# The gates of a final block in two turns of 128 nodes on one PSUM bank, and a fourth bank for the count products

## The chip, the core and the metric

The kernel runs on one core of a Trainium2 chip. The metric is the device time of one execution in microseconds (us), as the median of several runs; lower is better.

## The reference

One round of message passing over a graph of 12,500 nodes and 200,000 edges, a GRU cell, a residual and a layer normalization. The edges are sorted by destination, and the destinations are skewed: `dst = 12500 * u**2` with u uniform, so the first nodes have many edges each and the last ones few.

```python
src_h = h[src] @ W_msg.T + b_msg                       # h is x, [12500, 128] f32
msg = src_h + edge_embed[clip(edge_type, 0, 8)]
messages = segment_sum(msg, dst, 12500)
gi = messages @ W_ih.T + b_ih                          # [12500, 384], chunks r, z, n
gh = h @ W_hh.T + b_hh
r = sigmoid(i_r + h_r); z = sigmoid(i_z + h_z)
n = tanh(i_n + r * h_n)
h_new = (1 - z) * n + z * h
out = layernorm(x + h_new)
```

## The kernel before

The products with the weights are moved behind the sum over edges, so each node needs only the sum of its sources' rows of x and a count of its edge types. Two methods build the sums.

**Dense part (nodes 0 to 3327).** For each slot of 128 edges VectorE (DVE) writes two one-hot tables, `ohk` and `ohl` (lines 862 to 872, four slots at a time, "B" in the item list), and TensorE (PE) multiplies them into a count matrix in the PSUM tile `psb` (line 1082). A bank of `psb` holds the counts of four nodes; there are 832 such fillings, and they go round `NB = 3` banks. ScalarE (ACT) evicts each to SBUF (line 1213), and PE may only begin a filling when the one three before it is evicted (semaphore `s_eb`, line 1081). PE then multiplies the counts with all of x ("F", line 1097, bank `psf`), a block of 128 nodes in 49 pieces; "S", "T" and "C" reduce, transpose and copy the result.

**Sparse part (the other edges).** POOL gathers one tile of 128 rows of x per indirect DMA into a ring of 23 tiles (line 604). A group "G" is four tiles: PE multiplies them with one-hots (lines 1061 or 1065, and 1069) into the bank `psg`, and the last product adds 4 to the semaphore `s_used`. DVE adds `psg` to a ring of sums ("GA", line 891) when `s_used` tells that the group is done, and directly behind that it writes the one-hots of the group after next (lines 844 and 846). POOL waits for the same `s_used` before it writes a ring tile again (line 603), and PE waits for the GA of the group before (line 1056). There are 191 groups.

**Final blocks.** 49 blocks of 256 nodes get their GRU cell and norm in stages: `cn` (counts copied, DVE), `hh` (x times W_hh, PE, line 1026), `su` (sums and counts times the folded W_ih, PE, lines 1040 and 1043), `rz` (one Sigmoid over both halves, ACT, line 1190), `t2` (r times h_n, plus i_n, DVE, lines 798 and 799), `th` (Tanh, ACT, line 1193), `yt`, `bn`, `sd`, `ln`, and a store. The four gates of 128 nodes fill one PSUM bank, so a block of 256 takes both banks of `pAB`, one for each half.

**What sets the order.** Each engine runs strictly through one list, `ITEMS`, that `schedule` (line 193) makes. It goes through the groups; for each it lays down "G", then a chunk of one B or F item and GA, then further B and F items at a set pace. `STEPS = (3, 4)` steps of the final stages are spread evenly over the group's chunks: three while dense work is left, four after it. `SLOTS` (line 168) says which stages a step issues: a block has nine steps, so it takes three groups, and the next one starts when it is done. The first step of a group stands in the first chunk, behind GA. DVE prepares the one-hots of B slots 8 slots ahead of their place (line 919), and those of a group two groups ahead.

## Time and profile before

| | us |
|---|---|
| median of 3 runs | 1285.8 |
| lowest and highest of them | 1283.81 and 1469.57 |
| the profiled execution, its own time | 1292.56 |
| its span (first to last instruction) | 1290.4 |

A page of the profile gives the busy time of each engine: PE matmul, PEld (PE's weight loads), DVE, ACT and POOL. Waiting and semaphore instructions do not count as busy. In a timeline a row is a run of equal instructions: its start, its busy time, its engine, line, operation and tiles, and in square brackets how long the engine was idle before it and what ended that. "remote" and "issue" are ends for which the profile has no instruction to name. Recorded starts of PE are those at which an instruction was let go; the ends are modelled.

### The profile page before, as it was taken

The page shows a single profiled execution, that of the slowest core. Times are in us where ns is not written, and L with a number is a line of the kernel's source. Part 1 is how long each engine was busy: PE and PEld are TensorE (multiplying, and loading weights), DVE is VectorE, ACT ScalarE, POOL GpSimd, SP SyncE. Part 2 cuts the span into 40 slices and gives each one's busy share as a digit, 9 for nine tenths or more (in the row PEclk, how much of TensorE's full clock was granted, in tenths as well). Part 3 has the DMA queues.
Part 4 walks back from the last instruction along what each step waited for, and adds up shares of the span by engine and source line. Part 5 has one row for each costly group of instructions (what it writes and reads, how often), then busy time and mean ns, then how long its engine had stood idle before and what let it go on. Part 6 is the DMA issues. An engine that isn't in the chain of part 4 may idle for free.

```text
span 1290.4 us, 23001 instructions
## 1 busy us (share of the span) xinstructions
PE 1011.8 (78%) x8241; PEld 634.0 (49%) x8241; DVE 846.6 (66%) x2672; ACT 626.9 (49%) x1215; POOL 758.1 (59%) x807
## 2 busy tenths in 40 slices
PE   5535587888888887878888787888888787988794
PEld 1114354555545454555555554555555555555462
DVE  7503557667776676766777667767677677667644
ACT  4342314355545464545655556545565465555523
POOL 7725546565665666566656666656666666566640
PEclk9666588898999999999999999999999999999998
DMA  7629212222323223322323323323333332233331
GB/s 232 177 65 334 74 34 61 75 74 77 78 77 90 73 79 80 90 75 79 90 78 80 87 78 85 82 74 90 79 88 84 84 90 77 79 86 89 84 87 31
DMA packets 95665, 116.97 MB, mean 91 GB/s; under 512 B 20027, under 2 KB 81271, under 8 KB 95544
## 3 DMA queue, kind: packets, MB, share of 16 engines
q0 software_dynamic: 36608, 75.94, 22.1%
q1 hardware_dynamic: 57080, 37.80, 10.0%
q10 hardware_dynamic: 1856, 1.68, 0.5%
q8 instruction: 68, 1.11, 0.4%
q14 instruction: 53, 0.43, 0.1%
HBM read 99.34 MB, written 16.00 MB: 89 GB/s over the span
## 4 chain that ended last, share of the span: by engine, by line
PE 51%; DVE 18%; issue 13%; another core or an unknown queue 9%; ACT 6%; DMA 1%; SPq 1%; DVEq 0%; ACTq 0%
PE psf L1097 20%; PE psb L1082 12%; DVE ohk L862 4%; PE pAB L1026 4%; DVE ohl L868 4%; PE psg L1065 3%; PE pAB L1040 3%; DVE ohk L865 2%; PE psg L1061 2%; ACT mem L1213 2%; PE psg L1069 2%; DVE ohs L844 2%; PE pAB L1043 1%; DMA arena<-in_x 1%
## 5 line engine op out<-in xcount | busy, mean ns | idle before, releaser
L604 POOL DMA_INDIRECT xg<-x_split,idx x676 | 640.8, 948 | 405.4 <-remote 161.1
L1097 PE MATMUL psf<-mem 128*128 128x384 bf16 x2548 | 585.2, 334 | 11.5 <-issue 6.2
L1213 ACT CAST mem<-psb 128x432 f16<-128x432 f32 x832 | 392.9, 524 | 412.0 <-PE psb L1082 286.4
L1082 PE MATMUL psb<-ohk,ohl 128*128 128x108 bf16 (+3 forms) x1801 | 401.1, 263 | 143.4 <-issue 89.5
L862 DVE TENSOR_TENSOR ohk<-table_bank,prm 128x392 bf16<-128x392 f16 (+3 forms) x421 | 260.6, 619 | 113.3 <-PE psb L1082 70.7
L1082 PEld LDWEIGHTS psb<-ohk,ohl 128*128 128x128 bf16 x1801 | 167.7, 100 | 315.8 <-issue 163.7
L1097 PEld LDWEIGHTS psf<-mem 128*128 128x128 f16 x2548 | 223.6, 100 | 108.1 <-issue 30.7
L891 DVE TENSOR_TENSOR mem<-mem,psg 128x120 f32 (+10 forms) x191 | 56.7, 297 | 210.5 <-remote 159.2
L868 DVE TENSOR_TENSOR ohl<-table_bank,prm 128x512 bf16<-128x512 f16 x421 | 174.3, 414 | 0.0
L604 POOL DMA_INDIRECT xg<-in_x,idx x88 | 84.2, 957 | 76.0 <-PE psg L1069 39.7
L865 DVE TENSOR_TENSOR ohk<-table_bank,sort 128x40 bf16<-128x40 f16 (+3 forms) x421 | 102.5, 244 | 0.0
L1065 PE MATMUL psg<-ohs,xg 128*128 128x56 bf16 (+9 forms) x2028 | 97.7, 197 | 4.5 <-issue 4.3
L1065 PEld LDWEIGHTS psg<-ohs,xg 128*128 128x128 bf16 x2028 | 88.2, 98 | 20.7 <-issue 7.6
L844 DVE TENSOR_TENSOR ohs<-rel,table_bank 128x240 f32<-128x240 f16 (+10 forms) x191 | 83.4, 437 | 0.9 <-DVE flag L752 0.8
L1026 PE MATMUL pAB<-whh,xb 128*128 128x384 f32 x188 | 73.8, 516 | 0.2 <-issue 0.2
L1190 ACT ACTIVATE arena<-pAB 128x512 f32<-128x512 f32 x47 | 28.1, 597 | 71.7 <-PE pAB L1043 56.8
L1190 ACT ACT_TABLE_LOAD x48 | 61.6, 1283 | 0.9
L1198 ACT ACT_TABLE_LOAD x48 | 61.6, 1283 | 0.9
L1069 PE MATMUL psg<-ohs,tohb 128*128 128x60 bf16 (+10 forms) x764 | 58.7, 199 | 3.9 <-issue 3.9
L1040 PE MATMUL pAB<-wihc,mem 128*128 128x384 f32 x140 | 52.5, 494 | 2.9 <-issue 1.6
L1193 ACT ACTIVATE arena<-arena 128x256 f32<-128x256 f32 x47 | 19.6, 417 | 57.2 <-DVE arena L799 39.7
L1061 PE MATMUL psg<-ohs,xg 128*128 128x52 f32 (+1 forms) x176 | 33.3, 351 | 15.2 <-issue 15.2
(148 smaller groups left out, 827.0 us busy)
## 6 DMA issues: line engine op xcount, KB each, us to landing
xg<-x_split,idx POOLq DMA_INDIRECT x676
x_split<-mem SPq DMA_DIRECT2D x24, 384.0 KB
xb<-in_xT SPq DMA_DIRECT2D x49, 128.0 KB
arena<-in_x SPq DMA_DIRECT2D x24, 256.0 KB
arena<-in_xN SPq DMA_DIRECT2D x47, 128.0 KB
out<-arena SPq DMA_DIRECT2D x18, 128.0 KB
out<-spill SPq DMA_DIRECT2D x17, 128.0 KB
out<-spill SPq DMA_DIRECT2D x112, 8.0 KB
```

Source lines behind the costliest of these rows:

```text
L604: pool.indirect_dma_start(out=xg[:, p % RING, :] if split else xg32(p % RING), out_offset=None, in_=x_d if split else x, in_offset=bass.In ...
L844: v.tensor_tensor(onehots(g)[0], rel[:, g, :].unsqueeze(2).to_broadcast([P, G, w]), count_up[:, 0:w].unsqueeze(1).to_broadcast([P, G, w]), ...
L862: v.tensor_tensor(nodes[:, :, :, HT:HC], numbers[:, :, HT:HC].unsqueeze(1).to_broadcast([P, k, m, HI]), key[:, a:a + k, :].unsqueeze(2).to ...
L865: v.tensor_tensor(nodes[:, :, :, 0:HT], numbers[:, :, HT:2 * HT].unsqueeze(1).to_broadcast([P, k, m, HT]), sort[:, a:a + k].unsqueeze(2).u ...
L868: v.tensor_tensor(ohl[:, a % KB:a % KB + k, :].rearrange("p k (c t) -> p k c t", t=2), count_up[:, 0:P].rearrange("p (c t) -> p c t", t=2) ...
L1026: ins = pe.matmul(pAB[:, s, H:4 * H], xb[:, i % 2, s * P:(s + 1) * P], whh[:, :], start=True, stop=False, skip_group_check=True)
L1040: pe.matmul(pAB[:, s, 0:3 * H], sums[:, s * P:(s + 1) * P], wihc[:, :], start=False, stop=False, skip_group_check=True)
L1065: ins = pe.matmul(g2[:, 0, 0:w], xg[:, p % RING, c * H:(c + 1) * H], oh16[:, j, :], start=(j == 0 and c == 0), stop=(j == G - 1 and c == 2 ...
L1082: ins = pe.matmul(psb[:, bank % NB, held * HC:(held + m) * HC], ohl[:, e % KB, :], ohk[:, e % KB, d * HC:(d + m) * HC], start=(k == 0), st ...
L1097: pe.matmul(psf[:, 0:3 * H], Bb[q % 2][0:kk, HT + h, :], xs[0:kk, h, :, :].rearrange("p c f -> p (c f)"), start=(h == 0), stop=(h == HI - ...
L1190: act.activation(rz[:, :, :], pAB[:, :, H:3 * H], ACT.Sigmoid).then_inc(S["s_rz"], 1)
L1213: act.copy(Bb[q % 2][:, :, n:n + MOST], psb[:, bank % NB, 0:MOST * HC].rearrange("p (d h) -> p h d", h=HC)).then_inc(S["s_eb"], 1)
```

## The change

The gates of 256 nodes are worked off in two turns of 128 on one bank. `pAB` has one bank, and the bank that is free goes to `psb`, whose count products rotate over `NB = 4`. The stages `hh`, `su`, `rz` and `t2` become `hh0`, `su0`, `rz0`, `t20` and `hh1`, `su1`, `rz1`, `t21`; `hh1` writes the bank that `t20` has read, so PE waits at it for DVE. `th` and what follows stay whole. A block has twelve steps, there are four in a group (five after the dense part), so it still takes three groups, and the blocks come in the same order. Two of the last three blocks keep the old stages and take two banks of `psb`.

DVE's tables of B slots are prepared a little later where PE's items would else wait in a ring with `t20`. The first F item waits for the folded weights, as a product of theirs now uses `psf`. The three banks of the kernel's first stage and of its turns are other ones, as many as before.

```diff
-NB = 3
+NB = 4
-STEPS = (3, 4)
+STEPS = (4, 5)
-SHIFT = 5
+SHIFT = 8
+WIDE_SHIFT = 5
...
-SLOTS = (("cn",), ("hh",), ("su", "rz"), ("t2", "th", "zero"), ("yt",), (), ("bn",), ("sd",), ("ln",))
+SLOTS = (("cn",), ("hh0",), ("su0", "rz0"), ("t20",), ("hh1",), ("su1", "rz1"), ("t21", "th", "zero"), ("yt",), (), ("bn",),
+         ("sd",), ("ln",))
+WIDE = ("hh", "su", "rz", "t2")
+WIDE_SLOTS = (("cn",), ("hh",), ("su", "rz"), ("t2", "th", "zero"), ("yt",), (), ("bn",), ("sd",), ("ln",))
...
-        pAB = pb("pAB", [P, 2, 512])
-        xbank = [pAB[:, 0, :], pAB[:, 1, :], psf[:, :]]
+        pAB = pb("pAB", [P, 1, 512])
+        xbank = [pAB[:, 0, :], psf[:, :], psb[:, NB - 1, :]]
...
-                if kind == "t2":
-                    v.wait_ge(S["s_rz"], i + 1)
-                    v.wait_ge(S["s_pm"], i + 1)
-                    link(v.tensor_tensor(tn[:, 0, :, :], pAB[:, :, 3 * H:4 * H], rz[:, :, 0:H], ALU.mult))
-                    v.tensor_tensor(tn[:, 1, :, :], tn[:, 0, :, :], pAB[:, :, 0:H], ALU.add).then_inc(S["s_t2"], 1)
+                if kind[:2] == "t2":
+                    _, h, n = part_of(kind)
+                    v.wait_ge(S["s_rz"], 2 * i + h + n)
+                    v.wait_ge(S["s_pm"], 2 * i + h + n)
+                    link(v.tensor_tensor(tn[:, 0, h:h + n, :], pAB[:, :, 3 * H:4 * H], rz[:, h:h + n, 0:H], ALU.mult))
+                    v.tensor_tensor(tn[:, 1, h:h + n, :], tn[:, 0, h:h + n, :], pAB[:, :, 0:H], ALU.add
+                                    ).then_inc(S["s_t2"], n)
...
-                            ahead.setdefault(own[a - back] if a >= back else ("G", 0), []).append(it)
+                            e = it[1] - KB + min(OB, SLOTS_N - it[1]) - 1
+                            at = ("B", max(own[a - back][1], min(t for t in TOLD if t >= e))) if a >= back else ("G", 0)
+                            ahead.setdefault(at, []).append(it)
...
-                if kind == "hh":
-                    if second(i, slow) and not gone(i, slow):
+                parts, h, n = part_of(kind)
+                if kind[:2] == "hh":
+                    if h:
+                        pe.wait_ge(S["s_t2"], 2 * i + 1)
+                    elif second(i, slow) and not gone(i, slow):
                         pe.wait_ge(S["s_eb"], BANKS)
...
                             if q == 0:
                                 pe.wait_ge(S["s_xl"], UNITS)
+                                pe.wait_ge(S["s_wc"], 1)
...
-                    act.activation(rz[:, :, :], pAB[:, :, H:3 * H], ACT.Sigmoid).then_inc(S["s_rz"], 1)
+                    act.activation(rz[:, h:h + n, :], pAB[:, :, H:3 * H], ACT.Sigmoid).then_inc(S["s_rz"], n)
```

Two places show the order, both around group 99, with which `su` of node block 27 stood. On PE, before: `psg` is the group's bank, `pAB` the gates, `psb` the counts, `psf` the F products.

```order
L1065 MATMUL psg<-ohs,xg 128x72 x12
L1069 MATMUL psg<-ohs,tohb 128x72 x4
L1082 MATMUL psb<-ohk,ohl 128x108
L1040 MATMUL pAB<-wihc,mem 128x384 x2
L1043 MATMUL pAB<-emw,cnts 128x512 x2
L1082 MATMUL psb<-ohk,ohl 128x108
L1097 MATMUL psf<-mem 128x384 x2
```

The same place on PE in the changed kernel (line 1055 is `hh`, 1070 and 1073 are `su`, 1095 and 1099 the group).

```order
L1070 MATMUL pAB<-wihc,mem 128x384
L1073 MATMUL pAB<-emw,cnts 128x512
L1112 MATMUL psb<-ohk,ohl 128x108 x2
L1128 MATMUL psf<-mem 128x384 x2
L1095 MATMUL psg<-ohs,xg 128x72 x12
L1099 MATMUL psg<-ohs,tohb 128x72 x4
L1112 MATMUL psb<-ohk,ohl 128x108 x2
L1128 MATMUL psf<-mem 128x384 x2
L1112 MATMUL psb<-ohk,ohl 128x108
L1055 MATMUL pAB<-whh,xb 128x384
L1128 MATMUL psf<-mem 128x384 x2
```

Half of `su` moved ahead of the group's products, and `hh1` stands three B items and an F item behind them.

On DVE, before (line 891 is GA, 844 and 846 are the one-hots of group 101, 862 to 868 those of four B slots, 798 and 799 are `t2`):

```order
L891 TENSOR_TENSOR mem<-mem,psg 128x2x72
L844 TENSOR_TENSOR ohs<-rel,table_bank 128x288
L846 TENSOR_TENSOR tohb<-typ,table_bank 128x72
L862 TENSOR_TENSOR ohk<-table_bank,prm 128x4x98
L865 TENSOR_TENSOR ohk<-table_bank,sort 128x4x10
L868 TENSOR_TENSOR ohl<-table_bank,prm 128x512
L798 TENSOR_TENSOR arena<-pAB,arena 128x256
L799 TENSOR_TENSOR arena<-arena,pAB 128x256
```

On DVE in the changed kernel (913 is GA, 866 and 868 the group's one-hots, 819 and 820 are `t2`):

```order
L913 TENSOR_TENSOR mem<-mem,psg 128x2x72
L866 TENSOR_TENSOR ohs<-rel,table_bank 128x288
L868 TENSOR_TENSOR tohb<-typ,table_bank 128x72
L819 TENSOR_TENSOR arena<-pAB,arena 128x128
L820 TENSOR_TENSOR arena<-arena,pAB 128x128
L884 TENSOR_TENSOR ohk<-table_bank,prm 128x4x98
L887 TENSOR_TENSOR ohk<-table_bank,sort 128x4x10
L890 TENSOR_TENSOR ohl<-table_bank,prm 128x512
L819 TENSOR_TENSOR arena<-pAB,arena 128x128
L820 TENSOR_TENSOR arena<-arena,pAB 128x128
```

The first half of `t2`, for which `hh1` waits on PE, stands directly behind GA and the group's one-hots; the second half stands later in the same group, behind four more B slots.

## Rows read from the trace of the kernel before

**Rows 1.** The page, busy us by engine: TensorE's row.

```profile
PE 1011.8 (78%) x8241; PEld 634.0 (49%) x8241; DVE 846.6 (66%) x2672; ACT 626.9 (49%) x1215; POOL 758.1 (59%) x807
```

**Rows 2.** Waits: engine, tile, line <- releaser: us in total, times, longest.

```profile
PE psb L1082 <- issue: 89.5, 96, 2.3
PE psb L1082 <- ACT mem L1213: 16.7, 23, 2.1
...
POOL xg L604 <- remote: 172.4, 121, 2.6
```

**Rows 3.** Timeline of POOL, four gathers and the next one, and a run of eight.

```profile
407.29 0.94 POOL L604 DMA_INDIRECT xg<-x_split,idx  x1 [1.34 <-remote]
...
411.04 0.94 POOL L604 DMA_INDIRECT xg<-x_split,idx  x1 [0.30 <-issue]
413.45 0.94 POOL L604 DMA_INDIRECT xg<-x_split,idx  x1 [1.47 <-remote]
...
841.68 0.95 POOL L604 DMA_INDIRECT xg<-x_split,idx  x1 [0.30 <-issue]
```

**Rows 4.** Windows: stretch, length, busy us (instructions) of PE, PEld, DVE, ACT, POOL.

```profile
218.77:1246.33 1027.56, 858.80 (x7454) 547.07 (x7453) 715.83 (x2272) 539.23 (x1056) 629.50 (x664) 0.97 0.30 82
```

**Rows 5.** Timeline behind a group's products, 1110 to 1115 us.

```profile
1110.39 0.32 PE L1069 MATMUL psg<-ohs,tohb 128*128 128x84 bf16 x4
...
1112.04 0.95 POOL L604 DMA_INDIRECT xg<-x_split,idx  x1 [0.30 <-issue]
1112.17 0.49 PE L1097 MATMUL psf<-mem 128*128 128x384 bf16 x2
1114.13 1.36 ACT L1213 CAST mem<-psb 128x432 f16<-128x432 f32 x3 [2.54 <-remote]
...
1114.70 0.31 PE L1082 MATMUL psb<-ohk,ohl 128*128 128x324 bf16 x1 [2.05 <-issue]
1114.85 0.80 PE L1097 MATMUL psf<-mem 128*128 128x384 bf16 x2
```

**Rows 6.** Windows around that pause; the number behind POOL's is the granted clock.

```profile
1111.50:1114.90 3.40, 1.35 (x10) 0.62 (x9) 1.23 (x6) 0.86 (x3) 1.75 (x3) 1.00 0.22 64
1114.90:1118.30 3.40, 3.40 (x10) 1.91 (x9) 3.33 (x12) 1.11 (x3) 2.49 (x4) 0.50 0.25 63
```

**Rows 7.** Timeline of group 99 and of the block whose `su` stands behind it.

```profile
717.24 0.30 PE L1069 MATMUL psg<-ohs,tohb 128*128 128x72 bf16 x4
...
717.42 1.52 PE L1040 MATMUL pAB<-wihc,mem 128*128 128x384 f32 x4
718.08 0.95 POOL L604 DMA_INDIRECT xg<-x_split,idx  x1 [0.30 <-issue]
718.48 0.93 PE L1043 MATMUL pAB<-emw,cnts 128*128 128x512 f32 x2
...
720.19 0.36 DVE L862 TENSOR_TENSOR ohk<-table_bank,prm 128x392 bf16<-128x392 f16 x1 [2.58 <-remote]
...
720.90 0.29 DVE L891 TENSOR_TENSOR mem<-mem,psg 128x144 f32 x1
721.11 0.45 DVE L844 TENSOR_TENSOR ohs<-rel,table_bank 128x288 f32<-128x288 f16 x1
...
721.48 0.22 DVE L846 TENSOR_TENSOR tohb<-typ,table_bank 128x72 bf16<-128x72 f16 x1
...
722.68 0.30 PE L1069 MATMUL psg<-ohs,tohb 128*128 128x72 bf16 x4
...
724.14 0.94 POOL L604 DMA_INDIRECT xg<-x_split,idx  x1 [0.30 <-issue]
```

**Rows 8.** Groups by shape: count, busy us, mean ns of one.

```profile
L1026 PE MATMUL pAB<-whh,xb 128*128 128x384 f32 x188 | 73.8, 516 | 0.2 <-issue 0.2
L1190 ACT ACTIVATE arena<-pAB 128x512 f32<-128x512 f32 x47 | 28.1, 597 | 71.7 <-PE pAB L1043 56.8 <-remote 12.7 <-issue 2.0
L891 DVE TENSOR_TENSOR mem<-mem,psg 128x128 f32 x18 | 5.1, 286 | 18.9 <-remote 14.3 <-PE psg L1069 4.7
```

More of the change, by code:

```diff
@@ L164, in slot_table @@
     return [[t[j * P + p] for t in (thr, off, end, keys) for j in range(J)] for p in range(P)]
-STAGES = ("cn", "hh", "su", "rz", "t2", "th", "yt", "bn", "sd", "ln")
-SLOTS = (("cn",), ("hh",), ("su", "rz"), ("t2", "th", "zero"), ("yt",), (), ("bn",), ("sd",), ("ln",))
+STAGES = ("cn", "hh0", "su0", "rz0", "t20", "hh1", "su1", "rz1", "t21", "th", "yt", "bn", "sd", "ln")
+SLOTS = (("cn",), ("hh0",), ("su0", "rz0"), ("t20",), ("hh1",), ("su1", "rz1"), ("t21", "th", "zero"), ("yt",), (), ("bn",),
+         ("sd",), ("ln",))
+WIDE = ("hh", "su", "rz", "t2")
+WIDE_SLOTS = (("cn",), ("hh",), ("su", "rz"), ("t2", "th", "zero"), ("yt",), (), ("bn",), ("sd",), ("ln",))
+SECOND = (NBLK - 3, NBLK - 1)
 def dense_units():
@@ L190, in dense_units, with slots_of, shift_of @@
     return units + late
+def slots_of(i):
+    return WIDE_SLOTS if i in SECOND else SLOTS
+def shift_of(i):
+    return WIDE_SHIFT if i in SECOND else SHIFT
 def schedule():
@@ L220, in step @@
         else:
-            free = len(active) < 2 and (not active or done >= SECOND[0] or len(SLOTS) - len(active[-1]) >= SHIFT - 1)
+            free = len(active) < 2 and (not active or done >= SECOND[0] or len(slots_of(done - 1)) - len(active[-1]) >= shift_of(done - 1) - 1)
         b = pick(g, top) if free and done < NBLK - 1 else None
@@ L224, in step @@
             slots = [[(s, done, b) for s in slot if s != "zero" or b >= CB0]
-                     for slot in SLOTS]
+                     for slot in slots_of(done)]
             if b >= CB0:
@@ L228, in step @@
                 if b + 1 < NBLK and (BN * (b + 1) - ND) % R == 0:
-                    slots[5].append(("wrap", b + 1))
+                    slots[slots_of(done).index(())].append(("wrap", b + 1))
             done += 1
@@ L272, in schedule @@
     return items, lb, ub, late
-SECOND = (NBLK - 3, NBLK - 1)
 ITEMS, LB, UB, LATE = schedule()
 WG = [width(g) for g in range(GROUPS)]
-ORDER = [it[2] for it in ITEMS if it[0] == "hh"]
+ORDER = [it[2] for it in ITEMS if it[0] in ("hh", "hh0")]
+for kinds in (("hh0", "hh1", "hh"), ("su0", "su1", "su"), ("rz0", "rz1", "rz"), ("t20", "t21", "t2")):
+    turns = [(it[1], it[0][2:]) for it in ITEMS if it[0] in kinds]
+    assert turns == sorted(turns)
 POS = {b: i for i, b in enumerate(ORDER)}
@@ L291, in updates_before @@
             start = n
-        if it[0] in ("cn", "su"):
-            out[(it[0], it[1])] = start
+        if it[0] in ("cn", "su", "su0"):
+            out[(it[0][:2], it[1])] = start
         out[it] = n
@@ L477, in buffers, with part_of @@
             return (pAB1, rz1, tn1, y1, xn1) if second(i, slow) else (pAB, rz, tn, y, xn)
+        def part_of(kind):
+            return (range(2), 0, 2) if len(kind) == 2 else (range(int(kind[2]), int(kind[2]) + 1), int(kind[2]), 1)
         def stats(i, slow):
@@ L765, in weights @@
                 link(v.tensor_tensor(line, line, rest, ALU.add))
-                more(v.tensor_scalar(line[0:ND2, 0:3 * H], pAB[0:ND2, 1, 0:3 * H], 1.0, None, ALU.mult))
+                more(v.tensor_scalar(line[0:ND2, 0:3 * H], psf[0:ND2, 0:3 * H], 1.0, None, ALU.mult))
                 link(v.memset(line[0:ND2, 3 * H:4 * H], 0.0))
@@ L988, in turn @@
                     i = 3 * a + c
-                    if i >= NB:
-                        pe.wait_ge(S["s_te"], i - NB + 1)
+                    if i >= NB - 1:
+                        pe.wait_ge(S["s_te"], i - NB + 2)
                     for j in range(j0, j1):
-                        ins = pe.matmul(psb[:, i % NB, (j - j0) * P:(j - j0 + 1) * P], pre[:, c, j, :], pid[:, :],
+                        ins = pe.matmul(psb[:, i % (NB - 1), (j - j0) * P:(j - j0 + 1) * P], pre[:, c, j, :], pid[:, :],
                                         start=True, stop=True, skip_group_check=True)
@@ L1024, in final @@
                     pe.wait_ge(s_x[i % 2], 16 * (i // 2 + 1))
-                    for s in range(2):
-                        ins = pe.matmul(pAB[:, s, H:4 * H], xb[:, i % 2, s * P:(s + 1) * P], whh[:, :], start=True, stop=False,
+                    for s in parts:
+                        ins = pe.matmul(pAB[:, s - h, H:4 * H], xb[:, i % 2, s * P:(s + 1) * P], whh[:, :], start=True, stop=False,
                                         skip_group_check=True)
-                    ins.then_inc(S["s_hh"], 1)
-                elif kind == "su":
+                    if h + n == 2:
+                        ins.then_inc(S["s_hh"], 1)
+                elif kind[:2] == "su":
                     if slow:
@@ L1113, in _ @@
                         weights()
-                    elif it[0] in STAGES:
-                        final(*it, False, BEFORE[(it[0], it[1])] if it[0] == "su" else 0)
+                    elif it[0] in STAGES + WIDE:
+                        final(*it, False, BEFORE[("su", it[1])] if it[0][:2] == "su" else 0)
             with pe.Else():
```

37 lines of the change are left out of this document (20 added, 17 removed).

## The prediction

> **What bounds the kernel now.** I read the page first, for the busiest engine, then the waits, to see what that engine lacks, then the timelines, to see whether those waits are what the time consists of. The page has TensorE busy for 78% of the span, and the others less [rows 1]. The waits say that PE, at the first product of a bank, lost 16.7 us to ACT's eviction and 89.5 us with no releaser named [rows 2]. The second is mostly the same wait, for it ends as an eviction ends. So some 106 us look like a lack of PSUM banks, and a fourth bank looks like the cure.
>
> POOL's timeline tells otherwise. Its gathers come in runs of four, 1.25 us apart, and after each run POOL idles for about 1.4 us: from 411.98 to 413.45, say [rows 3]. Such pauses are the 172.4 us in 121 waits of POOL, 1.42 us each [rows 2]. A period is 413.45 - 407.29 = 6.16 us, and from 218.77 to 1246.33 us, 664 gathers or 166 groups took 1027.56 us, which is 6.19 us per group [rows 4]. So nearly every group takes one run and one pause, whatever PE has to do in it. That is a loop: POOL waits until PE has told that a group is used, and four tiles are free again.
>
> Why is the pause constant? Group products that ended by 1110.71 in the record were heard of only when ACT, DVE and POOL all went on at about 1114.1, which is 1.1 us after POOL's fourth gather ended at 1112.99 [rows 5]. In group 99 the products ended at 717.54, the fourth gather at 719.03, and DVE went on at 720.19, again 1.1 us later [rows 7]. So what PE tells behind a group's products arrives 1.15 us after POOL's run of four, or at once if the products end later than that. PE's idle time behind a group is mostly this hold, not a lack of banks, and a PE that gets to the group earlier gains nothing. PE has busy 858.80 of 1027.56 us there [rows 4], so about 1.0 us of a group's 6.19 is slack.
>
> The Trainium skill (Advanced Engine Details and Errata, "DMA Bandwidth Details") puts a semaphore increment on trn2 at about one cycle. These rows do not agree: what is heard of a group is over 1 us late [rows 5, 7]. By that figure POOL would wait for PE alone; that is the third rival below.
>
> **The change part by part.**
>
> *The fourth bank.* It can only help where the loop is not what holds: the stretch before 218 us, the last 44 us, and the groups in which PE is later than POOL's run. The latter cost (6.19 - 6.13) x 166 = 10 us, taking 6.13 as a run of 4.70 and a pause of 1.43. Ends: 0, and 10 us plus some 15 us of the waits outside the loop. I take 13 us less.
>
> *The split.* The number of products stays. DVE does four operations of 128 columns for two of 256. The nearest row is 286 ns for one of 128x128 [rows 8], so some 0.3 us more per block, 14 us in all. ACT does two Sigmoids where one took 597 ns [rows 8], perhaps 0.25 us more. DVE is free 312 and ACT 488 of those 1027.56 us [rows 4], so neither is on the path: 0, and at most those 14 us.
>
> *The wait of `hh1`.* This is the term that decides. `hh1` waits for `t20`, and `t20` stands on DVE behind GA of the same group and two one-hots. GA waits for the held message. Queued behind `hh1` on PE are all products of the rest of the group and the next group's, and POOL, DVE and ACT wait for those. Take group 99 [rows 7]:
> - its products end at 717.54, and three B items and one F item come before `hh1`: about 0.5 us, so PE is there at 718.0;
> - GA starts at 720.90 (DVE first makes the table that waited till 720.19); with the one-hots it is done at 721.70; `t20` takes 2 x 0.29 = 0.6 us, and `hh1` goes at 722.35. PE has paused 4.3 us;
> - then PE needs 0.8 us for `hh1` (two products of 4 in the row, 516 ns with overlap) [rows 8], 1.0 for `su1` (half of 717.42 to 719.41), and the rest. In the kernel before `su` ended at 719.41 and group 100's products at 722.98: 3.6 us, less the 0.5 ahead of `hh1`, 3.1. So group 100 ends at 722.35 + 4.9 = 727.25;
> - POOL's run ends at 724.14 + 0.94 = 725.08, and until 726.23 a group is in time. It is 1.0 us late, and the loop slips by that. In the kernel before it had 2.1 us to spare against the run's end.
>
> The slip comes once per block, in the middle of its three groups; the next two can't win it back, as the loop has no shorter period. For 45 blocks inside the loop the ends are 0 (a group with few dense items, or a PE that the pause lets arrive no later) and 2 us (a heavy one). I take 0.9 us, a little under the example, which is a group of middling weight: 40 us.
>
> *The clock.* The pauses have a second price. A pause of 2.05 us [rows 5] in a stretch in which PE was busy 1.35 of 3.40 us was followed by 3.4 us at a granted clock of 0.50, the lower of the two levels (1.2 GHz), and two F products took 0.80 instead of 0.49 us [rows 5, 6]. PE then does half as much in 3.4 us, a loss of up to 1.65 us, and here it falls on the stretch that is already late. Not every such pause did this. Ends: 0, and 45 x 1.65 = 74 us. I take one block in three: 25 us.
>
> The Trainium skill (TensorE: Matmul & The Clock Gate, "HAM oscillation — how this bites in real kernels") speaks against this change twice. It says that idle gaps between bursts of products let the clock fall back, with which rows 6 agree, and that adding double buffering in PSUM to a kernel whose TensorE stayed busy gained nothing further. The sum above would be the same without it.
>
> *The rest.* Before the loop the first F item waits for the folded weights, at about 171 us instead of 168; PE then waited for DVE at 169 to 172 anyway. 1 us, ends 0 and 3. Tables of B slots are made up to two slots later: nothing, as DVE leads PE by eight; the end of that is a fraction of a us per group, inside the range. The last blocks keep their form.
>
> **Sum.** 40 + 25 + 1 - 13 = 53 us on the profiled execution's own 1292.56, so 1345.6. That execution stands 6.8 us above the median of 1285.8, so I forecast 1339 us. Its own range is 1312 to 1375.
>
> **The rivals.**
> - *The clock falls in every block.* For it: the pause in the example, 4.3 us, is twice the one of rows 5. Against it: as the loop slips PE arrives later at `hh1`, and the pause shortens. 1339 - 25 + 74 = 1388 us.
> - *The slip vanishes (ends on the other side).* Place: the message of the block's middle group. Once PE stands at `hh1` with nothing else let go, what it told may be heard before POOL's run ends. In that case GA, `t20` and `hh1` come about 1.1 us or more earlier, and POOL goes on without its pause. For it: at 841.68 a fifth gather followed the fourth after the usual 0.30 us [rows 3], so the message can come in time. Against it: in rows 5 PE was idle for 2.05 us and it did not come sooner. It decides from 1.0 us earlier on. Slip 0, clock 0 to 10, less 10: about 1286 us.
> - *There is no loop; banks bound the time.* Then the fourth bank gives half of the 106 us of rows 2, and `hh1` costs its pause only where DVE is behind: 45 x 0.4 = 18 us. 1286 - 53 + 18 = 1251 us. Against it: the constant period of rows 3 and 4. For it: only the page and the waits.
> - *The change does not do what it says.* The order shows that it does; the bank is free for all but the last blocks. I leave it out.
>
> **How the numbers follow.** The forecast has 0.54, the clock in every block 0.13, the vanished slip 0.25, no loop 0.08. A measurement of this kernel tells about 2% from no change, 26 us. Slower by more than that: 0.54 x 0.94 + 0.13 = 0.64. Faster by more: the 0.08. The rest, 0.28, is the same. The range reaches from the vanished slip to just short of the worst clock: 1285 to 1386, which leaves out the 0.08 and most of the 0.13. The likeliest case's own range, 1312 to 1375, lies inside it.
>
> **What would show it.** In the profile after I expect: a wait of PE at line 1055 for DVE line 820, near 45 times, some 2 to 4 us each; POOL's period still 6.1 to 6.2 us in two groups of three and about 7 us in the third; a mean period near 6.5 us; many more short stretches at clock 0.50, and a mean clock below 0.924; the waits at the bank's first product down from 106 us to under 50. The prediction is wrong if POOL's mean period stays at 6.2, if `hh1` waits under 1 us, or if the period falls below 6.0, which would mean that the loop is not what I take it for.

## The result and the profile after

The changed kernel took 1354.42 us (median of 4 runs, 1348.4 to 1361.34), the kernel before 1285.6: a ratio of 1.0542, with a 95% interval of 1.047 to 1.0614. It is slower by 69 us. The forecast was 1339 us. The ratios, here and below, are of fast runs, while a median is of all runs of a kernel, with those that fell in the slower state (1469.57 us once for the kernel before). Against the profiled executions' own times (1358.04 and 1292.56) the difference is 65.5 us, where the sum of the terms said 53.

The page of the changed kernel, TensorE's clock in 40 slices and the chain that ended last:

```profile
PE 1043.0 (77%) x8241; PEld 647.8 (48%) x8241; DVE 861.7 (64%) x2766; ACT 642.9 (47%) x1264; POOL 763.2 (56%) x807
...
PEclk8665578999899898999989989988899998899987
...
PE 45%; DVE 28%; issue 12%; another core or an unknown queue 11%; ACT 2%; DMA 1%; DVEq 1%; SPq 0%; ACTq 0%
```

PE is busy 31 us longer than in [rows 1] with the same 8241 products, so part of its work ran at the lower clock; the mean granted clock is 0.898 in place of 0.924. The waits (engine, tile, line <- releaser: us in total, times, longest):

```profile
PE pAB L1055 <- DVE arena L820: 102.5, 44, 4.7
...
PE psb L1112 <- issue: 36.6, 31, 5.5
...
PE pAB L1070 <- DVE cnts L804: 22.8, 20, 4.5
```

Three things are to be seen. The waits at a bank's first product, 106 us in [rows 2], have become 38.7 (36.6, and 2.1 for ACT): the fourth bank does what a look at the page alone would ask of it, and the kernel is slower. In their place PE waits at `hh1` (line 1055) for `t20` (line 820), 44 times, 2.33 us each. And 22.8 us at line 1070 are new (1.3 at line 1040 before): `su0` waits for the copied counts.

The same stretch as in [rows 4], and the place of [rows 7] in the changed kernel, around group 99:

```profile
218.77:1246.33 1027.56, 834.87 (x7052) 527.11 (x7051) 697.29 (x2253) 525.49 (x1052) 599.96 (x628) 0.94 0.29 77
```

```profile
741.98 0.95 POOL L624 DMA_INDIRECT xg<-x_split,idx  x1 [0.30 <-issue]
...
742.77 0.30 PE L1099 MATMUL psg<-ohs,tohb 128*128 128x72 bf16 x4
...
744.09 0.36 DVE L884 TENSOR_TENSOR ohk<-table_bank,prm 128x392 bf16<-128x392 f16 x1 [2.54 <-PE psb L1112]
...
744.29 0.95 POOL L624 DMA_INDIRECT xg<-x_split,idx  x1 [1.37 <-PE psg L1099]
...
744.81 0.29 DVE L913 TENSOR_TENSOR mem<-mem,psg 128x144 f32 x1
...
745.38 0.22 DVE L868 TENSOR_TENSOR tohb<-typ,table_bank 128x72 bf16<-128x72 f16 x1
...
745.84 0.29 DVE L820 TENSOR_TENSOR arena<-arena,pAB 128x128 f32<-128x128 f32 x1
746.18 0.91 PE L1055 MATMUL pAB<-whh,xb 128*128 128x384 f32 x2 [2.65 <-DVE arena L820]
...
748.05 0.95 POOL L624 DMA_INDIRECT xg<-x_split,idx  x1 [0.30 <-issue]
...
748.85 1.48 PE L1070 MATMUL pAB<-wihc,mem 128*128 128x384 f32 x2
...
752.50 0.30 PE L1099 MATMUL psg<-ohs,tohb 128*128 128x72 bf16 x4
...
753.07 0.95 POOL L624 DMA_INDIRECT xg<-x_split,idx  x1 [4.06 <-PE psg L1099]
```

628 gathers are 157 groups, so 6.54 us per group in place of 6.19. The second fence is the forecast's mechanism, link by link: the products of group 99 end at 743.07 (the last four, from 742.77, 0.30 us), DVE hears nothing until 744.09, which is 1.16 us after POOL's run ended at 742.93, GA comes at 744.81, one-hots and `t20` stand behind it, `hh1` goes at 746.18 after a pause of 2.65 us, and POOL, whose run ended at 749.0, pauses 4.06 us in place of 1.4. The clock fell right behind the pause (PE was busy for all of the second stretch, at a granted clock of 0.50):

```profile
744.30:747.10 2.80, 0.92 (x4) 0.50 (x5) 1.79 (x8) 0.31 (x1) 2.19 (x3) 1.00 0.34 92
747.10:750.52 3.42, 3.42 (x11) 1.74 (x9) 0.80 (x3) 0.52 (x1) 1.60 (x2) 0.50 0.36 86
```

All periods, sorted by where they stand in a block, give the sizes. From the starts of the POOL gathers that a group lets go, the mean period that ends with a block's first, second and third group (43 blocks each) was 6.09, 6.16 and 6.32 us before; after, it is 6.08, 6.21 and 7.67. So nearly all of the loss stands in the third group: 1.35 x 43 = 58 of the 65.5 us. Of the rest some 5 us stand at the end: from the gather that group 184 lets go to the last instruction the kernels took 44.09 and 49.22 us. Up to the one that group 26 lets go they took 270.06 and 270.55, so the fourth bank made the part ahead of the 43 blocks no shorter. Of the 43 third periods, 23 have a stretch of clock 0.50 in them and last 8.39 us in the mean; the 20 without one last 6.83, where such periods lasted 6.23 before. Hence a slip of 0.60 us in those 20, and 1.56 us more in the 23. The 1.56 are not the clock's alone: PE's pause at `hh1` was 2.73 us in the mean of the 23, and 1.67 in the 20.

### The profile page after: what moved, and what is told of

It is laid out like the page before. It is cut to its first block, busy times and chain, and to the rows that moved or that the text cites. A ratio compares the mean times of both kernels' runs of the same rounds, so it can differ in the third digit from the quotient of the medians.

```text
span 1356.2 us, 23328 instructions
## 1 busy us (share of the span) xinstructions
PE 1043.0 (77%) x8241; PEld 647.8 (48%) x8241; DVE 861.7 (64%) x2766; ACT 642.9 (47%) x1264; POOL 763.2 (56%) x807
## 4 chain that ended last, share of the span: by engine, by line
PE 45%; DVE 28%; issue 12%; another core or an unknown queue 11%; ACT 2%; DMA 1%; DVEq 1%; SPq 0%; ACTq 0%
PE psf L1128 15%; PE psb L1112 8%; DVE ohk L884 5%; PE pAB L1070 5%; PE pAB L1055 5%; DVE ohl L890 4%; DVE ohs L866 4%; PE psg L1099 3%; DVE ohk L887 3%; PE psg L1095 2%; PE psg L1091 2%; DVE mem L913 2%; PE pAB L1073 1%; DVE tohb L868 1%
## 5 line engine op out<-in xcount | busy, mean ns | idle before, releaser
L1128 PE MATMUL psf<-mem 128*128 128x384 bf16 x2548 | 597.4, 338 | 10.0 <-issue 4.5
L1245 ACT CAST mem<-psb 128x432 f16<-128x432 f32 x832 | 398.2, 527 | 417.6 <-PE psb L1112 279.2
L1112 PE MATMUL psb<-ohk,ohl 128*128 128x108 bf16 (+3 forms) x1801 | 400.3, 266 | 66.4 <-issue 36.6
L1112 PEld LDWEIGHTS psb<-ohk,ohl 128*128 128x128 bf16 x1801 | 171.8, 102 | 220.9 <-issue 93.4
L913 DVE TENSOR_TENSOR mem<-mem,psg 128x120 f32 (+10 forms) x191 | 56.8, 297 | 193.1 <-remote 128.1
L1055 PE MATMUL pAB<-whh,xb 128*128 128x384 f32 x188 | 94.2, 586 | 103.8 <-DVE arena L820 102.5
L1222 ACT ACTIVATE arena<-pAB 128x256 f32<-128x256 f32 x94 | 36.1, 384 | 143.0 <-PE pAB L1073 65.7
L1070 PE MATMUL pAB<-wihc,mem 128*128 128x384 f32 x140 | 70.9, 593 | 27.3 <-DVE cnts L804 22.8
L1055 PEld LDWEIGHTS pAB<-whh,xb 128*128 128x128 f32 x188 | 32.6, 209 | 122.6 <-DVE arena L820 118.6
L1073 PE MATMUL pAB<-emw,cnts 128*128 128x512 f32 x94 | 74.2, 789 | 0.3 <-issue 0.3
```

Of the source, the lines that this page charges most:

```text
L1055: ins = pe.matmul(pAB[:, s - h, H:4 * H], xb[:, i % 2, s * P:(s + 1) * P], whh[:, :], start=True, stop=False, skip_group_check=True)
L1070: pe.matmul(pAB[:, s - h, 0:3 * H], sums[:, s * P:(s + 1) * P], wihc[:, :], start=False, stop=False, skip_group_check=True)
L1112: ins = pe.matmul(psb[:, bank % NB, held * HC:(held + m) * HC], ohl[:, e % KB, :], ohk[:, e % KB, d * HC:(d + m) * HC], start=(k == 0), st ...
L1128: pe.matmul(psf[:, 0:3 * H], Bb[q % 2][0:kk, HT + h, :], xs[0:kk, h, :, :].rearrange("p c f -> p (c f)"), start=(h == 0), stop=(h == HI - ...
L1222: act.activation(rz[:, h:h + n, :], pAB[:, :, H:3 * H], ACT.Sigmoid).then_inc(S["s_rz"], n)
L1245: act.copy(Bb[q % 2][:, :, n:n + MOST], psb[:, bank % NB, 0:MOST * HC].rearrange("p (d h) -> p h d", h=HC)).then_inc(S["s_eb"], 1)
```

## The experiments

The runs were made in three groups, each on one chip beside the kernel before. The record gives the chips the numbers 2 (the first four rows), 5 (the next four) and 2 again (the last four):

| kernel | us | before, same group | ratio [95% interval] |
|---|---|---|---|
| e1_bank3 | 1332.58 | 1271.67 | 1.0466 [1.0422, 1.051] |
| e2_hh1_later | 1284.65 | 1271.67 | 1.0039 [0.9986, 1.0092] |
| e5_runs8 | 1595.74 | 1271.67 | 1.2573 [1.2491, 1.2656] |
| e4_pertile | 1293.98 | 1271.67 | 1.0133 [1.007, 1.0196] |
| e9_wait | 1285.97 | 1287.34 | 0.9985 [0.9946, 1.0023] |
| e10_wait_all | 1320.58 | 1287.34 | 1.0221 [1.0158, 1.0285] |
| e6_half_before | 1121.12 | 1287.34 | 0.869 [0.8635, 0.8745] |
| e7_half_after | 1167.27 | 1287.34 | 0.9 [0.8944, 0.9057] |
| e12_after_again | 1094.83 | 1044.92 | 1.0478 [1.045, 1.0505] |
| e8_later_bank3 | 1095.96 | 1044.92 | 1.0488 [1.0461, 1.0516] |
| e3_t20_early | 1051.74 | 1044.92 | 1.0074 [1.0046, 1.0102] |
| e11_wait_early | 1096.63 | 1044.92 | 1.0502 [1.0468, 1.0536] |

The last group ran the same kernel before in 1044.92 us, 18% less than the first, which has the same chip number. Whether a number names the same chip in both, and what else differed, the record does not say. The difference matters for the reading and is taken up below.

For each kernel, the mean time from the end of one group's products to the end of the next group's, in us, for a block's first, second and third group (43 of each):

| kernel | first | second | third | sum |
|---|---|---|---|---|
| before | 5.19 | 6.76 | 6.74 | 18.69 |
| after | 4.81 | 6.79 | 9.11 | 20.71 |
| e1_bank3 | 4.81 | 6.71 | 8.68 | 20.20 |
| e2_hh1_later | 4.89 | 6.92 | 7.33 | 19.14 |
| e9_wait | 5.07 | 6.71 | 7.23 | 19.01 |
| e6_half_before | 4.18 | 5.31 | 6.09 | 15.58 |
| e7_half_after | 4.27 | 5.79 | 6.62 | 16.68 |
| e12_after_again (last group) | 4.26 | 5.76 | 6.63 | 16.65 |
| e3_t20_early (last group) | 4.27 | 5.80 | 5.66 | 15.73 |
| e8_later_bank3 (last group) | 4.51 | 6.08 | 5.87 | 16.46 |
| e11_wait_early (last group) | 4.15 | 5.31 | 7.34 | 16.80 |

### Is there a loop? (e5_runs8, e6_half_before)

```diff
-                    pool.wait_ge(S["s_used"], p - RING + 1)
+                    pool.wait_ge(S["s_used"], -(-(p - RING + 1) // 8) * 8)
```

> The kernel before, in which POOL waits for whole pairs of groups: its gathers come in runs of eight, in the same order and into the same ring. Nothing else changes, and PE never lacks a tile (it gathers four groups ahead). Theory (what PE tells is heard only 1.15 us after POOL's run has ended, and each group needs such a message before the next): a pair of groups takes a run of 9.7 us, the hold of 1.15, GA and nearly a whole group of PE, some 16 us, so 8 us per group in place of 6.19 and some 300 us more: about 1590 us (1450 to 1650). Rival (POOL just waits for PE, and its runs hold nothing): the time stays within 20 us of 1286.

Measured: 1595.74 us, 324 us more; 8.06 us per group (from the products of group 30 to those of group 185; 6.17 in the kernel before), where 8 was forecast. POOL's timeline shows the run of eight, and DVE's the two GA that belong to it:

```profile
855.30 0.95 POOL L604 DMA_INDIRECT xg<-x_split,idx  x1 [6.63 <-PE psg L1069]
...
864.08 0.95 POOL L604 DMA_INDIRECT xg<-x_split,idx  x1 [0.30 <-issue]
870.77 0.95 POOL L604 DMA_INDIRECT xg<-x_split,idx  x1 [5.74 <-PE psg L1069]
...
855.83 0.29 DVE L891 TENSOR_TENSOR mem<-mem,psg 128x144 f32 x1
...
866.80 0.30 DVE L891 TENSOR_TENSOR mem<-mem,psg 128x144 f32 x1 [4.65 <-remote]
```

The products of group 100 ended at 860.49, in the middle of the run. The run ended at 865.03, and GA began at 866.80, 6.3 us after its products. POOL gathers four groups ahead, so no tile was missing; a longer run held the message longer. Where POOL only waits for PE this edit would have cost nothing: the rival is out.

The hold can be counted in the trace of the kernel before. Of 145 waits of DVE of over 0.3 us between groups 29 and 180 that ended with PE or with no instruction to name, 116 ended 1.0 to 1.5 us after POOL's last gather of a run, though POOL is within a run three quarters of the time. 25 ended within a run, so some messages do get through.

```diff
-                    gather(p, True)
+                    if p < FULL or p % G < 2:
+                        gather(p, True)
...
-                            pe.wait_ge(s_g[p % RING], 16 * (p // RING + 1))
+                            if p < FULL or j < 2:
+                                pe.wait_ge(s_g[p % RING], 16 * landed(p))
```

`FULL` is the first tile that may be left out, and `landed` counts the gathers that a place of the ring has had.

> The kernel before, in which from the 29th group on POOL gathers only two of a group's four tiles; PE multiplies what the ring holds, so the sums of the sparse part are not the reference's. PE, DVE and ACT do all they did. Theory of the loop: POOL's run is 2.2 us in place of 4.7, what PE tells is heard at once or at most 3.4 us after the run began, and the period falls from 6.1 to what PE itself needs, 5.2 to 5.6 us: 85 to 140 us less, about 1155 us (1130 to 1190). Rival (PE, its banks and DVE set the period, POOL only follows): 1255 to 1272.

Measured: 1121.12 us, 166 us less (13.1%), at the fast end of what was expected. POOL's runs of two are short, and its message comes at once:

```profile
641.54 0.95 POOL L611 DMA_INDIRECT xg<-x_split,idx  x1 [1.04 <-PE psg L1078]
642.79 0.94 POOL L611 DMA_INDIRECT xg<-x_split,idx  x1 [0.30 <-issue]
646.98 0.95 POOL L611 DMA_INDIRECT xg<-x_split,idx  x1 [3.24 <-PE psg L1078]
```

The products of groups 99 and 100 ended at 641.27 and 646.71: 0.27 us before POOL went on, both times. With PE, ACT and DVE doing the same work the period fell from 6.17 to 5.12 us. In these groups of runs the loop, not PE and not the banks, sets the period.

### What the fourth bank is worth (e1_bank3)

```diff
+NC = 3
...
-                            if bank >= NB and held == 0 and k == 0:
-                                pe.wait_ge(S["s_eb"], bank - NB + 1)
+                            if bank >= NC and held == 0 and k == 0:
+                                pe.wait_ge(S["s_eb"], bank - NC + 1)
...
```

The products and the evictions take `bank % NC` in the same way.

> The changed kernel, in which the count products rotate over three banks and the fourth lies idle; all else is as changed. Theory of the loop (POOL's run of four gathers and the message of PE that is held behind it set the period): the fourth bank was worth only 13 us, so some 1367 us (1354 to 1380), POOL's period in two groups of three still 6.1 to 6.2 us. Rival (banks bound the time, and the fourth one gave half of the 106 us of waits at a bank's first product): some 1405 us.

Measured: 1.0466 times the kernel before; the changed kernel stood at 1.0542 in its own measurement (it was not run beside this one), and the intervals overlap. Without the fourth bank it is not slower, perhaps 0.7% faster. PE's waits in that kernel:

```profile
PE pAB L1056 <- DVE arena L821: 88.8, 42, 4.6
PE psb L1113 <- issue: 47.8, 49, 6.9
...
PE psb L1113 <- ACT mem L1246: 9.0, 14, 1.8
```

The waits at a bank are 56.8 us in place of 38.7, but those at `hh1` fall from 102.5 to 88.8. That fits a PE that is held back by a bank and comes later to `hh1`, which no run shows by itself. In the third group's interval the mean time at clock 0.50 was 1.69 us in place of 2.32. My 13 us for the fourth bank were wrong here; beside the pause at `hh1` its worth was 0, or a little below. What it is worth without that pause, where messages are held, was not measured: `e8_later_bank3`, meant for it, was run in the last group.

### Is it the pause at hh1? (e2_hh1_later, e3_t20_early)

```diff
-... ("t20",), ("hh1",), ("su1", "rz1"), ("t21", "th", "zero"), ("yt",), (), ("bn",),
+... ("t20",), (), ("hh1",), ("su1", "rz1"), ("t21", "th", "zero"), ("yt",), ("bn",),
```

> The changed kernel with the empty step of a block moved ahead of hh1, so that hh1, su1, rz1, t21, th and yt come one step (a quarter of a group) later on all engines, and t20 stays. Theory (the cost is the pause of PE at hh1 behind GA and t20, the slip and the low clock behind it): PE's waits at hh1 fall from 102 us to under 20, POOL's period in the block's third group falls from 7.67 to about 6.3 us, and the time by some 55 to 1300 us (1285 to 1315). Rival (two turns cost by their number: more instructions, more messages, or the waits of su0 on the copied counts): the time stays at 1340 to 1360.

Measured: 1.0039 times the kernel before (1284.65 us is the median of nine runs, by which it would be 1.0102). 5.0 of the 5.4% of the changed kernel's own measurement come back, with both turns, all their instructions and the new wait for the copied counts (22.2 us in 14 here) left in. The third group's interval falls from 9.11 to 7.33 us. PE's waits at `hh1` did not fall under 20 us, as forecast, but to 37.5 in 25, with 11.5 in 12 more that have no releaser named:

```profile
PE pAB L1055 <- DVE arena L820: 37.5, 25, 3.7
...
PE pAB L1070 <- DVE cnts L804: 22.2, 14, 4.6
```

A quarter of a group later PE often still stands there, for `t20` behind the held message; what is left of the waits costs little, by the ratio.

This is the run that speaks against the rival that two turns cost by their instructions. The other way to take the pause away leaves PE's order alone and moves `t20` ahead of GA on DVE:

```diff
-... ("su0", "rz0"), ("t20",), ("hh1",),
+... ("su0", "rz0", "t20"), (), ("hh1",),
```

> The changed kernel with t20 one step earlier, with su0 and rz0 at the end of the group before, ahead of GA on DVE; hh1 and all behind it stay where the change put them, a few items behind the group's products on PE. The other way to take the pause away: if it is the order on DVE (GA and two one-hots ahead of t20) that costs, PE's waits at hh1 fall from 102 us to under 15, and the time to within 1.5% of the kernel before. Rival 1: hh1 and su1 cost by standing right behind the group's products on PE, whatever DVE does: still 3 to 5% above. Rival 2: DVE now stands 1 to 2 us at t20 for the Sigmoid, and its tables come late for that: PE waits for ohl instead, and 2 to 4% above.

Measured, in the last group: 1051.74 us, 1.0074, where the changed kernel stood at 1.0478. PE's waits at `hh1` fell from 37.6 us to 2.9, the tables' (`ohl`) stayed (21.6 and 21.5). The third interval falls by 0.96 us, the other two stay. The same place in both, first the changed kernel, then this one (PE's products of group 99 end at 584.62 and 567.03):

```profile
584.33 0.30 PE L1099 MATMUL psg<-ohs,tohb 128*128 128x72 bf16 x4
...
585.42 0.29 DVE L913 TENSOR_TENSOR mem<-mem,psg 128x144 f32 x1
...
586.46 0.29 DVE L820 TENSOR_TENSOR arena<-arena,pAB 128x128 f32<-128x128 f32 x1
586.80 0.91 PE L1055 MATMUL pAB<-whh,xb 128*128 128x384 f32 x2 [1.71 <-DVE arena L820]
```

```profile
566.84 0.29 DVE L820 TENSOR_TENSOR arena<-arena,pAB 128x128 f32<-128x128 f32 x1
...
567.33 0.87 PE L1055 MATMUL pAB<-whh,xb 128*128 128x384 f32 x2
...
567.83 0.29 DVE L913 TENSOR_TENSOR mem<-mem,psg 128x144 f32 x1
```

`hh1` stands where it stood and goes without a pause, ahead of GA. Both of the expectation's rivals are out, for a group of runs in which nothing is held: the place right behind the group costs nothing, and DVE's stand at `t20` for the Sigmoid did not make the tables late.

### The wait alone (e9_wait, e10_wait_all, e11_wait_early)

```diff
+            if len(seen) == 4 and SWITCH <= g < GROUPS - AHEAD and (every or g == begun + 1):
+                out[it] = g
...
+                    if it in STALLS:
+                        pe.wait_ge(S["s_oh"], STALLS[it] + AHEAD)
```

The tables of B slots are made later, as in the changed kernel. `seen` are the B and F items since the group's products, `begun` is the group with the block's `hh`; `every` is False in the first and True in the second.

> The kernel before with one wait more and nothing else of the change (the tables of B slots are made up to two slots later, as in the changed kernel, so that the wait can't end in a ring): in 43 groups, those behind the group in which a block's hh stands, PE waits at the fourth B or F item behind the group's products for the one-hots that DVE makes directly behind GA. No instruction is added, all banks and stages are as before. Theory: this wait alone makes PE pause (it ends about 0.6 us sooner than the changed kernel's wait for t20), and brings most of the slip and of the low clock: 20 to 50 us more, about 1307 us where the kernel before takes 1272. Rival (two turns cost by their instructions): within 5 us of the kernel before.

> The same wait in every group, 164 in place of 43. Theory: each group then slips. PE goes on about 2.0 us after POOL's run has ended, or 1.2 us after its own message where that came later, and has some 5 us of work from there to the next group's end: a period of 6.8 to 7.2 us in place of 6.1, so 110 to 180 us more, about 1410 us. Rival: within 5 us of the kernel before.

Both missed. `e9_wait` measured 0.9985, no difference where 20 to 50 us were forecast, and so the rival's figure; that rival, that two turns cost by their instructions, is out by `e2_hh1_later` and `e3_t20_early`, which have them all. `e10_wait_all` measured 1.0221, 28 us where 110 to 180 were forecast; its interval, 1.0158 to 1.0285, is clear of no change. So no wait added to the kernel before gave the loss of the changed one in these groups of runs. PE's waits for the one-hots, of the first and of the second:

```profile
PE psf L1116 <- DVE tohb L863: 19.0, 13, 2.4
...
PE psb L1101 <- DVE tohb L863: 9.6, 10, 2.2
```

```profile
PE psf L1116 <- DVE tohb L863: 102.9, 63, 3.7
PE psb L1101 <- DVE tohb L863: 51.8, 38, 2.9
PE psb L1101 <- issue: 28.2, 30, 8.3
```

In `e9_wait` 20 of the 43 waits were none, and the other 23 took 1.24 us: the wait stands behind `su`, whose products (717.42 to 719.41, 2.0 us, in [rows 7]) cover most of it. In the changed kernel half of `su` has moved ahead of the group and the other half behind the wait, so that its pause is 2.33 us and has no cover. In `e10_wait_all` 101 waits took 1.53 us each, 155 us in all, of which only 28 showed: PE's waits at a bank with no releaser named fell to 28.2 (79.6 in `e9_wait`), as PE stood elsewhere for the same message. I had added pauses to the period as if each were new; here most of them took the place of others.

```diff
-            if len(seen) == 4 and
+            if len(seen) == 1 and
```

> e9_wait again, but with its 43 waits at the first item behind the group's products, ahead of su, where e9_wait had su's four products (2.4 us) ahead of the wait, so that 20 of its 43 waits were none and the others took 1.24 us. Theory: a pause costs what it exceeds the slack of 1.0 us in a group by, and the low clock behind it. These should take some 2.7 us each, 43 x 1.7 = 73 us and some 10 for the clock, less what PE would have waited behind the group anyhow: 3.5 to 6.5% above the kernel before, with no instruction added. Rival (pauses behind a group's products are made up for, as in e9_wait, and the two turns cost in another way): under 1%.

Measured, in the last group: 1.0502, 52 us more, with no instruction added; PE waits 43.0 us in 42. This agrees with the forecast in the total and not in the pause: 1.0 us each, in place of 2.7 less a slack of 1.0. In this group nothing is held (below), and the pauses count in full, with some 9 us beside them. What this wait would cost where messages are held was not tried, so `e9_wait` and this run do not tell whether the place of the wait or the missing hold makes the difference.

```profile
PE pAB L1059 <- DVE tohb L863: 43.0, 42, 2.0
```

### The message by tiles (e4_pertile)

```diff
-                        for j in range(G):
                             ins = pe.matmul(g2[:, 1, 0:w], tohb[:, g % AHEAD, j * ND2:j * ND2 + P], oh16[:, j, :], start=False,
                                             stop=(j == G - 1), skip_group_check=True)
-                        ins.then_inc(S["s_used"], G)
+                            ins.then_inc(S["s_used"], 1)
```

> The kernel before, in which PE tells each of a group's four tiles when it has used it (the products of a tile's edge types stand behind its other three, and each adds 1 to the count), in place of one message of 4. Theory of the hold: POOL starts its run about 1 us earlier with one gather, the three others follow when that gather's hold is over (0.94 + 1.15 us), and the last message of the group is heard then too, some 3.5 us earlier than when it is held behind a run of four. PE no longer waits for the group's message, but POOL's own period becomes 0.94 + 1.15 + 0.3 + 3.45 + 1.15, about 7 us: near 1400 us. If a message of a tile gets through between two gathers instead, both waits go and the period falls to what PE is busy, 5.2 to 5.7 us: 1200 us. Rival (no hold): 1286 less at most 15 us.

Measured: 1.0133, 22 us more by the medians, neither of the two outcomes forecast. POOL's runs stayed runs of four: the four messages of a group stand within the 0.7 us of its products, so if one falls into a run, all do, and they are let go together. This run does not tell the theories apart.

### The change without the hold (e7_half_after, e12_after_again, e8_later_bank3)

> The changed kernel with the same half of the gathers, to be read against the last run. Theory: with no message held for long, hh1 still waits for GA, the one-hots and t20, some 1.3 us in place of 2.3, and PE now is the bound, so every such pause counts in full, less what the fourth bank gives back: 10 to 50 us more than the last run, 1165 to 1205. The extra over the kernel before is smaller than the 69 us of the full kernels. Rival (the change's cost has nothing to do with POOL's loop): the full 69 us more.

The edit is that of `e6_half_before`, and the same half of the gathers is left out. Measured: 0.900 times the full kernel before, where `e6_half_before` had 0.869, so some 40 us more (46 by the medians). The pause at `hh1` is shorter, as expected:

```profile
PE pAB L1063 <- DVE arena L828: 37.7, 42, 4.0
```

0.90 us each in place of 2.33. The pauses are down by 65 us, but the cost falls only from 69 to some 40 us: with the loop's slack gone, 37.7 us of pauses cost about what they last.

> The changed kernel once more, beside which the three others are read. It should stand 4.7 to 6.1% above the kernel before, as in its first measurement.

1.0478: as expected. The surprise is the time, 1094.83 us. POOL's timeline around the same group 99:

```profile
583.75 0.95 POOL L624 DMA_INDIRECT xg<-x_split,idx  x1 [0.30 <-issue]
...
587.52 0.95 POOL L624 DMA_INDIRECT xg<-x_split,idx  x1 [0.30 <-issue]
588.77 0.94 POOL L624 DMA_INDIRECT xg<-x_split,idx  x1 [0.30 <-issue]
592.01 0.95 POOL L624 DMA_INDIRECT xg<-x_split,idx  x1 [2.30 <-PE psg L1099]
```

No pause stands after four gathers, and GA (585.42, shown above) comes in the middle of a run, 0.8 us after its group's products. The 28 GA between groups 27 and 184 for which DVE stood idle (over 0.3 us) began 0.15 us after their products; the 97 of the kernel before did so 2.66 us after, in the median. In `e3_t20_early` 597 of the last 654 gathers stand in one run. In this group of runs what PE tells is not held back, and PE's waits at a bank with no releaser named are gone. The table agrees: `e7_half_after`, with short runs where long ones hold, has the intervals of `e12_after_again`, with full runs where nothing is held (4.27, 5.79, 6.62 and 4.26, 5.76, 6.63).

So most of the change's cost needs neither the hold nor the low clock, which stands in none of the 43 third intervals here: `e12_after_again` costs 50 us, with 37.6 us of pauses at `hh1`.

```diff
-... ("t20",), ("hh1",), ("su1", "rz1"), ("t21", "th", "zero"), ("yt",), (), ("bn",),
+... ("t20",), (), ("hh1",), ("su1", "rz1"), ("t21", "th", "zero"), ("yt",), ("bn",),
...
-                            if bank >= NB and held == 0 and k == 0:
+                            if bank >= NC and held == 0 and k == 0:
```

The rest of the edit is that of `e1_bank3`.

> e2_hh1_later with the count products on three banks, the fourth idle: two turns and the kernel before's number of banks, without the pause. As e1_bank3 showed the fourth bank worth nothing beside the pause, the question is whether it is worth something without it. The prediction's size: 13 us more than e2_hh1_later, so 1.4% above the kernel before. Theory as it stands now (the loop sets the period, so a PE that may run ahead only waits longer): equal to e2_hh1_later, 0 to 0.9% above the kernel before. Rival (banks bound): 4% above.

Measured: 1.0488, the rival's side, which the expectation had put at 4%. `e2_hh1_later`, to which it was to be compared, was not run in this group. Against `e3_t20_early` it is 44 us slower. PE's waits:

```profile
PE psb L1113 <- ACT mem L1246: 18.9, 38, 1.3
...
PE pAB L1056 <- DVE arena L821: 8.1, 11, 1.4
```

At a bank's first product PE waits 18.9 us for ACT, with four banks 0.7; at `hh1` 8.1 in place of 2.9; and it is busy 966.5 us in place of 949.1. These make 41 of the 44 us. The two kernels differ in the places of `hh1` and `t20` too, so how much of it is the bank's is not shown; the waits at a bank alone are 18 us more. Where messages are held, `e1_bank3` found nothing.

## Why the prediction was right

**The loop and the hold: right, and shown.** `e5_runs8` and `e6_half_before` put the period where the hold says, 8.06 and 5.12 us, from both sides of 6.17. What the prediction took for a property of PE's messages is not always there: the last group of runs had none of it, and the kernel before took 18% less time there. The Trainium skill (Advanced Engine Details and Errata, "DMA Bandwidth Details") puts the overhead of a semaphore increment at about one cycle, among details of the DMA engines. It gives no time until another engine hears of one, so the held messages do not speak against it, as the prediction had it, and the 0.15 us of the last group are not a measure of it.

**The wait of `hh1`: right in place, in count and in mechanism; the slip taken too large.** The expected signs came: 44 waits for line 820, 2.33 us each (45 of 2 to 4 us); nearly all of the loss in a block's third group; a mean period of 6.54 us (6.5); a mean clock of 0.898 (below 0.924); waits at a bank of 38.7 us (under 50). Two ways of taking the pause away, in two groups of runs, gave back 5.0 of 5.4% and 4.0 of 4.8%. The example of group 99 had put its pause at 4.3 us; it was 2.65, since the group's products ended 0.1 us after POOL's run and not 1.5 us before it; that agrees with what the prediction held against its first rival, that PE arrives later at `hh1` and the pause shortens. Where the clock did not fall the slip was 0.60 us per block and not 0.9, which would make 26 us of all blocks in place of 40. And the pause costs without the hold too (40 us in `e7_half_after`, 50 in `e12_after_again`), which the prediction did not say.

**The clock: right in kind, mis-sized in number.** It fell in 23 of 43 blocks and not in one of three. The periods with a fall were 1.56 us longer, near the 1.65 worked out; 36 us in place of 25, if all of it were the clock's. But their pauses were 1.06 us longer as well, so this is the most that it can be by this count, and the slip's share is larger if it is less.

**The fourth bank: the term that failed.** 13 us were to come back; where messages are held `e1_bank3` found 0 or a small loss. Of the two places where the gain was to be, the stretch ahead of the 43 blocks took the same time (270.06 and 270.55 us), and so did the 29 groups among the blocks that belong to none (6.13 and 6.14 us). In the blocks the fewer waits at banks and the longer ones at `hh1` suggest that the pause takes the gain away again; that is not shown apart.

**The sum.** Slip and clock were to be 40 + 25 = 65 us, and the third groups lost 58, some 7 less. The rest of the kernel lost 7.5 us, 5 of them at its end, where 1 was put down, and the bank's 13 did not come. That makes the 12 us by which the forecast of 53 was short of 65.5. The number of falls was taken too small and the slip too large; these two errors went against each other, which is luck, so the total is better than its parts.

**The rivals.** "The clock falls in every block": no, in about half. "The slip vanishes": no; PE standing at `hh1` did not bring its message forward. "There is no loop, banks bound the time": out in the first two groups of runs. In the last, though, nothing is held, and the change is not faster there as that rival had it, but 4.8% slower: its 18 us for the pauses of `hh1` were 43, the difference of `e12_after_again` and `e3_t20_early`. Why `e3_t20_early`, which hardly waits at a bank, still stands 0.7% above the kernel before stays open, for no profile of the kernel before was taken in that group. There was little left to win: its gathers follow each other without a pause, 4 x (0.95 + 0.30) = 5.0 us per group, and its groups took 5.17 (from group 30 to group 185).

No version tried beats the kernel before. The two best, `e2_hh1_later` and `e3_t20_early`, come to within 0.4 and 0.7% of it.

## What to carry to other kernels

A step that waits for another engine costs what stands ahead of the releasing instruction in that engine's queue. Before a buffer is halved and its work taken in two turns, find in both queues what stands between the release and the reuse, and move the release ahead (here `t20` ahead of GA) or the reuse back by a step. And a wait that a profile books on a resource (106 us at PSUM banks here) is worth what an experiment gives when the resource is added or taken away: here, with a closed loop behind it, taking the fourth bank away cost nothing. What a pause costs depends on what stands beside it: 23 waits of 1.24 us behind two us of products cost nothing, and 42 of 1.0 us with nothing ahead of them, in another group of runs, cost 52 us.

## What the runs showed of the hardware

- PE's messages were mostly held while POOL issued gathers, in the profiles before and after and in the first eight runs: with runs of eight the GA for which DVE stood idle began 4.75 us after their products in the median and 7.6 at most; 6.3 in the example. In the last group they were not held: such GA began 0.15 us after their products in the median. The same kernel took 1044.92 us there, and 1271.67 and 1287.34 us in the other two. What makes the difference is open; the record has chip number 2 on both sides of it, and the gathers took 0.95 us with 0.30 between them on both.
- In the profile of the changed kernel PE's granted clock fell to 0.50 (1.2 GHz) in 23 of 43 third periods, with a mean pause at `hh1` of 2.73 us, and stayed there for 3.4 us in the example; 20 periods with a mean pause of 1.67 us had no fall. In the last group, with pauses of 0.8 us in the mean, it fell in none of the 43 third intervals.
